# Squares taken one unit ahead, inverse roots spread over the scan, and gates stored in the scan's order

## The chip, the cores and the metric

The kernel runs on one core of a Trainium2 chip. The metric is the device time of one execution in microseconds. The times shown are the median of three runs; the profile is of one further execution, taken by the hardware profiler.

## What is computed

The input x is 16 sequences of 256 tokens with 256 features. The model has four parts in a row; the change lies in the first.

1. RMS norm of x, a causal convolution of 4 taps over the tokens with SiLU, projections to queries, keys and values of 16 heads of 16 features, and to two gates per head, beta and alpha. Then the gated delta rule, a recurrence over the tokens:

```
S = a[..., None, None] * S
pred = einsum('bhkv,bhk->bhv', S, k)
S = S + k[..., :, None] * (b[..., None] * (v - pred))[..., None, :]
o = einsum('bhkv,bhk->bhv', S, q)
```

2. An output projection, a second RMS norm, a gated MLP and a layer norm.
3. Cross attention to a context of 120 tokens per sequence, and a layer norm.
4. Eight experts, one for each token, and a layer norm.

## The kernel before, in words

The program is written by hand for five engines with semaphores; each engine runs its own list of instructions in order. There are three stages: `front_and_scan`, `scan_and_post`, and the experts.

**Units.** The work ahead of the recurrence is cut into NU = 16 units. A unit is 4 sequences of 64 tokens; U = 4 units cover all sequences for one part of 64 tokens, and there are PARTS = 4 parts. A unit goes through these steps: SyncE loads x (`load_rows`); ScalarE squares and sums it (line 638, into ss); GpSimd makes the inverse root (`inverse_rms`, lines 450 and 452); ScalarE scales x by it (line 645; VectorE does so for units 0 to 3, line 531); TensorE transposes; ScalarE writes the result with the norm's weight (line 666); TensorE convolves (line 795; VectorE for units 0 to 3); ScalarE applies SiLU (line 653); TensorE projects; ScalarE moves the projections to st and stores them to the DRAM tensor qkv (lines 678 and 680), then the gates to bst (line 690), and the gates are stored with four small DMAs (`store_gates`, line 342): by GpSimd for units 0 to 3, by ScalarE for the others. ScalarE's list is software-pipelined: `step(a, b, c)` treats the scale and transposition of unit a, the SiLU of unit b = a - 1 and the projections of unit c = a - 2.

**Raw loads.** SyncE's `load_raw(part, h)` brings keys, queries, gates and values of one part and one half h of the sequences from DRAM into the order of the scan, after it has waited for each of their stores. The gates take eight DMAs per half (line 379). For part 1 the two halves stand behind `load_rows` of units 9 and 10. The loads of parts 2 and 3 stand behind the 16 contexts (`contexts`, keys and values of the cross attention), and those behind unit 15.

**Lengths.** `lengths(some, h)` makes the inverse norms of keys and queries and the scales from the gates. It is shared by ScalarE (squares of keys and of queries, line 712; sigmoid, lines 703 and 704; roots) and VectorE (sums of the squares, line 559; products; reciprocals). `some` is 0 for part 0, 1 for part 1, 2 for parts 2 and 3.

**Scan.** VectorE walks the recurrence over 128 tokens at a time (jb = 0, then jb = 1), in CHUNKS = 16 chunks of R = 8 tokens. A token takes four instructions for each half of the sequences (lines 159, 170, 181, 191). At the sixth token of each chunk (u = 5) `next_scales` copies the next scales (line 125), so this copy marks the chunks in the trace. Beside it GpSimd reads out: `read_out(c, z, h)` covers four tokens of one half with one product (line 246), three folds (line 252) and one more (line 254). A chunk has four read-outs, two for each z, and one product of the queries (line 230). VectorE may overwrite the state of a slot only when GpSimd has read it eight tokens before (semaphore S_read, waited for at line 191 for every fourth token). VectorE's chunks 5 and 6 hold the sums of `lengths(1, h)`, the keys' from the second token on, and chunks 14 and 15 those of `lengths(2, h)`.

**Where the units lie.** GpSimd's list sets when a unit's inverse root is made, since it stands between read-outs. Written as (chunk, z), units 4 and 5 stand ahead of the scan; units 6 to 11 behind (0,0), (0,1), (1,0), (1,1), (2,0), (2,1); unit 12 behind (3,0); units 13, 14 and 15 behind (7,0), (7,1) and (8,0). ScalarE has `lengths(1, 0)` and `lengths(1, 1)` behind step 2U + 4 = 12.

Of the kernel before, what the change touches and what calls it, by code (L numbers as in the profile page):

```python
# [14 lines left out]
P = 128  # L15
# [7 lines left out]
NU = PARTS * U  # L23
R, Q, V, KN, KB = 8, 4, 4, 4, 2
# [239 lines left out]
def front_and_scan(nc, sem, w, k, s, arena):  # L264
# [4 lines left out]
    with ExitStack() as ctx:  # L269
# [6 lines left out]
        xt = sb("xt", [P, 2, 2, D])  # L276
        ss, ms, rstd = (sb(n, [P, 2, 2]) for n in ("ss", "ms", "rstd"))
# [23 lines left out]
        ct, cT = sb("ct", [CTX, 2, D]), sb("cT", [P, 2, G, CTX])  # L301
# [4 lines left out]
        pa = ps("pa", [P, G, 2 * TB])  # L306
        pc = pp[:, 0, :, 0:CTX]
# [5 lines left out]
        x_in, ct_in, kv_out = ([sem(f"f_{n}{i}") for i in range(2)] for n in ("x_in", "ct_in", "kv_out"))  # L313
# [18 lines left out]
        SETUPS = 13  # L332
        TAPS = KC * G
# [3 lines left out]
        def store_gates(eng, n):  # L337

            eng.wait_ge(evac_done, n * 4 + 4)
            for i in range(2):  # L340
                for g in range(G):
                    eng.dma_start(k["gates"][i, n, g].rearrange("a q h t -> h (a q) t"),
                                  bst[32 * i + g * H // G:32 * i + (g + 1) * H // G]).then_inc(gates_out[n >= U], 16)

        @block.sync
        def _(sp):
            def load_rows(n):

                part, u, s = n // U, n % U, n % 2
                if n >= 2:  # L350
                    sp.wait_ge(xn_done, (n - 1) * 2)
# [14 lines left out]
            def load_raw(part, h):  # L366
# [5 lines left out]
                for i, name, dst in ((1, "k", x["k"]), (0, "q", x["q"]), (3, None, None), (2, "v", x["vo"])):  # L372

                    if i == 3:
                        later = part > 0
                        sp.wait_ge(gates_out[later], 64 * (units - U * later))
# [50 lines left out]
        def _(pool):  # L427
# [18 lines left out]
            def inverse_rms(a):  # L446
                if a:
                    n, slot, m = a
                    pool.wait_ge(ss_done, (n + 1) * 2)
                    nc.gpsimd.tensor_tensor(ms[:, slot], ss[:, slot], k["eps"][:, 0], ALU.add).then_inc(rstd_done, 1)  # L450
                    pool.wait_ge(rstd_done, n * 2 + 1)
                    nc.gpsimd.tensor_tensor(rstd[:, slot], ms[:, slot], k["exponent"][:], ALU.pow).then_inc(rstd_done, 1)
# [1582 lines left out]
```

## Time and profile before

| | before |
|---|---|
| median of 3 runs | 1869.99 us |
| lowest and highest | 1865.32 and 1873.29 us |
| the profiled execution's own time | 1867.18 us |
| its span in the trace | 1865.5 us |
| TensorE busy | 1325.9 us, 71% |
| VectorE busy | 1254.0 us, 67% |
| GpSimd busy | 1000.8 us, 54% |
| ScalarE busy | 849.6 us, 46% |
| mean granted TensorE clock | 0.854 |

The span is the time from the first to the last instruction in the trace. Busy times are of one engine over the whole span, with stages of different limits in it, so they do not tell which engine sets the time of a stage. A row of the trace gives the start, the duration, the engine, the line, what is written and read, and in brackets how long the engine stood idle before it and what ended that. Consecutive instructions of one kind are merged into one row with a count. PE is TensorE, DVE VectorE, ACT ScalarE, POOL GpSimd; SPq and ACTq are DMA issues of SyncE and ScalarE.

### The profile page before, as it was taken

The numbers are of one execution on the slowest core, as the hardware profiler recorded it, in microseconds if no ns is written. First come the engines' busy times: TensorE is split into PE (matmuls) and PEld (weight loads), VectorE is DVE, ScalarE is ACT, GpSimd is POOL, SyncE is SP. The second block draws the span as 40 slices with busy tenths as digits, with TensorE's granted clock in tenths as the row PEclk, the third lists the DMA queues.
The fourth block names the chain that finished last, engine by engine and source line by source line (L and its number), as shares of the span: only waits on it lengthen the run. The fifth ranks groups of instructions, "written<-read, shape, count | busy, mean of one in ns | idle before, by whom it ended". The sixth has DMA issues, their size and how long they took to land. (4 is left out here: it accounts for less than half of the span.)

```text
span 1865.5 us, 32852 instructions
## 1 busy us (share of the span) xinstructions
PE 1325.9 (71%) x9000; PEld 1151.7 (62%) x9001; DVE 1254.0 (67%) x3301; ACT 849.6 (46%) x2808; POOL 1000.8 (54%) x1234
## 2 busy tenths in 40 slices
PE   6277106850036676766765899998489999999997
PEld 4265105630025465654654778876389999999997
DVE  3798999999988999999876144454434444443442
ACT  5433213442113665667766488887322322322332
POOL 3367868987669999998866324342111122122121
PEclk9689558885568878878877999998789999999999
DMA  5344001566031010100002111133130410411200
GB/s 139 74 102 111 12 6 42 143 173 95 23 120 38 23 33 18 32 27 27 28 27 84 57 42 52 54 120 120 40 103 21 154 48 22 158 42 45 77 17 7
DMA packets 182719, 119.29 MB, mean 64 GB/s; under 512 B 124849, under 2 KB 163560, under 8 KB 182120
## 3 DMA queue, kind: packets, MB, share of 16 engines
q1 hardware_dynamic: 119848, 90.98, 17.4%
q10 hardware_dynamic: 58864, 18.71, 4.0%
q0 software_dynamic: 3920, 8.60, 1.3%
q8 instruction: 34, 0.56, 0.1%
q14 instruction: 53, 0.43, 0.1%
HBM read 83.44 MB, written 35.74 MB: 64 GB/s over the span
## 5 line engine op out<-in xcount | busy, mean ns | idle before, releaser
L246 POOL TENSOR_TENSOR wt<-wt 128x1024 f32<-128x1024 f32 x128 | 301.5, 2355 | 53.9 <-DVE wt L191 46.9
L252 POOL TENSOR_TENSOR wt<-wt 128x512 f32<-128x512 f32 (+2 forms) x384 | 307.6, 801 | 30.1
L1942 PE MATMUL e_ph<-e_g,e_w 128*128 128x128 f32 x2496 | 285.2, 275 | 0.7 <-ACT e_g L1912 0.7
L1942 PEld LDWEIGHTS e_ph<-e_g,e_w 128*128 128x128 f32 x2496 | 281.9, 192 | 0.9 <-issue 0.9
L191 DVE SCALAR_TENSOR_TENSOR wt<-wt,scan 128x256 f32<-128x256 f32 x512 | 242.0, 473 | 18.0 <-POOL wt L246 13.4
L170 DVE TENSOR_REDUCE wt<-wt 128x16 f32<-128x272 f32 x512 | 219.2, 428 | 0.1
L181 DVE TENSOR_TENSOR scan<-wt,scan 128x256 f32<-128x256 f32 x512 | 215.0, 420 | 0.3
L159 DVE TENSOR_TENSOR wt<-wt,scan 128x256 f32<-128x256 f32 x512 | 210.1, 410 | 0.9 <-PEq L269 0.5
L1420 ACT ACTIVATE wt<-p_pX,p_mx 128x120 f32<-128x120 f32 x512 | 176.4, 387 | 71.9 <-DVE p_mx L1205 70.3
L1903 ACT ACTIVATE e_g<-e_ph,wt 128x128 f32<-128x128 f32 x156 | 48.7, 363 | 304.9 <-PE e_ph L1942 304.9
L1821 POOL TENSOR_TENSOR e_ve<-e_mv,eps 128x1 f32<-128x1 f32 x39 | 7.4, 190 | 327.1 <-DVE e_mv L1877 327.1
L1554 PE MATMUL p_pm<-p_w_mix,p_oT 128*128 128x256 f32 x128 | 43.7, 500 | 160.6 <-DMA p_oT<-o 129.9
L1953 PE MATMUL e_ph<-e_xT,e_w 128*128 128x128 f32 x1248 | 148.3, 278 | 0.6 <-DVE e_xT L1858 0.6
L1953 PEld LDWEIGHTS e_ph<-e_xT,e_w 128*128 128x128 f32 x1248 | 145.0, 195 | 1.0 <-issue 1.0
L782 PE MATMUL f_pT<-ident,f_xn 128*128 128x128 f32 x64 | 15.0, 377 | 171.9 <-ACT f_xn L645 157.9
L1554 PEld LDWEIGHTS p_pm<-p_w_mix,p_oT 128*128 128x128 f32 x128 | 30.8, 252 | 170.4 <-issue 162.0
L1205 DVE TENSOR_REDUCE p_mx<-p_pX 128x8 f32<-128x960 f32 x64 | 72.9, 1150 | 75.7 <-PE p_pX L1600 75.5
L1420 ACT ACTIVATION_READ_ACCUMULATOR wt<-p_pX,p_mx 128x1 f32 x512 | 119.9, 234 | 0.0
L782 PEld LDWEIGHTS f_pT<-ident,f_xn 128*128 128x128 f32 x64 | 9.7, 188 | 177.4 <-ACT f_xn L645 162.8
L1912 ACT ACTIVATE e_g<-e_ph,wt 128x128 f32<-128x128 f32 x312 | 97.4, 363 | 42.0 <-PE e_ph L1953 41.8
L1850 DVE COPY e_w<-wt 128x4096 f32 x39 | 89.5, 2295 | 27.3 <-issue 22.2
L1566 PE MATMUL p_pX<-p_hT,p_wg 128*128 128x256 f32 x320 | 94.8, 424 | 16.7 <-ACT wt L1420 16.6
(226 smaller groups left out, 2925.0 us busy)
## 6 DMA issues: line engine op xcount, KB each, us to landing
wt<-in_L_ffn_W SPq DMA_DIRECT2D x24, 1024.0 KB
qkv<-f_st ACTq DMA_DIRECT2D x48, 256.0 KB, 2.6
p_kE<-kE SPq DMA_DIRECT2D x16, 480.0 KB, 3.7
p_vP<-vP SPq DMA_DIRECT2D x16, 480.0 KB
wt<-qkv SPq DMA_DIRECT2D x12, 512.0 KB, 6.4
e_xt<-routed ACTq DMA_DIRECT2D x39, 130.0 KB, 2.1
f_xt<-in_x SPq DMA_DIRECT2D x32, 128.0 KB, 2.8
p_oT<-o SPq DMA_DIRECT2D x16, 256.0 KB
```

The source lines that it names most:

```text
L159: nc.vector.tensor_tensor(s["sk"][:, h, u % V, :, 0:HD], s["S"][:, h, (u - 1) % R], s["kn"][:, h, u % KN:u % KN + 1].to_broadcast([P, HD, ...
L170: nc.vector.tensor_reduce(s["w"][:, h], s["sk"][:, h, u % V], AX, ALU.add).then_inc(s["w_done"], 1)
L181: nc.vector.tensor_tensor(s["outer"][:], s["w"][:, h].rearrange("p (v o) -> p v o", o=1).to_broadcast([P, HD, HD]), s["kn"][:, h, u % KN:u ...
L191: nc.vector.scalar_tensor_tensor(s["S"][:, h, u], s["S"][:, h, (u - 1) % R], s["gate"][:, jb, h, 2, bass.ds(c * R + u, 1)], s["outer"][:], ...
L246: nc.gpsimd.tensor_tensor(x, s["S"][:, h, z * Q:(z + 1) * Q], s["qn"][:, h, z * Q:(z + 1) * Q].rearrange("p t (o d) -> p t o d", o=1).to_b ...
L252: nc.gpsimd.tensor_tensor(x[:, :, :, 0:half], x[:, :, :, 0:half], x[:, :, :, half:2 * half], ALU.add).then_inc(s["o_fold"][h], 1)
L1420: ins = nc.scalar.activation(pr[:, x // 2, head], scores(x)[:, y // 4, y % 4], ACT.Exp, bias=mx[:, x // 2, head:head + 1], accum_out=sm[:, ...
L1566: ins = nc.tensor.matmul(gu(i)[:, which], wt[:, g, i * P:(i + 1) * P], hT[:, g], start=(g == 0), stop=(g == G - 1))
L1850: nc.vector.tensor_copy(w2[:, s].rearrange("p c f -> p (c f)"), wt[:, bass.ds(at + W2_AT, C1 * F2)]).then_inc(w2_kept, 1)
L1912: nc.scalar.activation(g1[:, c], ph1[:, c // 2, c % 2], ACT.Gelu, bias=k["bias"][:, bass.ds(at + c * NE, 1)]).then_inc(g1_done, 1)
L1942: ins = nc.tensor.matmul(ph2[:, c // 2, c % 2], w2[:, s, i, c * P:(c + 1) * P], g1[:, i], start=(i == 0), stop=(i == C1 - 1))
L1953: ins = nc.tensor.matmul(ph1[:, c // 2, c % 2], w1[:, s, g, c * P:(c + 1) * P], xT[:, g], start=(g == 0), stop=(g == G - 1))
```

## The change

It has four parts.

- Squares go one unit ahead. A function `squares_of(n)` takes the place of the squares at the head of `step`; it is called for unit a + 1 behind the scaling of unit a. Its full-size output goes to a new PSUM tile `squared` and no longer to xn. The buffers of x and of its sums have XS = 3 slots in place of 2, and `load_rows` runs three units ahead. The context's buffer ct now lies in acc.
- Fewer inverse roots beside the scan's first chunks. Unit 4 stands behind (0,1), unit 5 behind (1,0), units 6 and 7 behind (2,0) and (2,1), unit 8 behind (3,0), units 9 and 10 behind (4,0) and (4,1), none in chunks 5 and 6, units 11 and 12 behind (7,0) and (7,1), unit 13 behind (8,0), units 14 and 15 behind (9,0) and (9,1).
- ScalarE's `lengths(1, 0)` and `lengths(1, 1)` come behind step 2U + 2 = 10.
- The DRAM tensor gates has its dimensions in the scan's order: eight stores of 4 KB for each unit, two loads of 64 KB for each half.

The core of the diff:

```diff
@@ store_gates
                 for g in range(G):
-                    eng.dma_start(k["gates"][i, n, g].rearrange("a q h t -> h (a q) t"),
-                                  bst[32 * i + g * H // G:32 * i + (g + 1) * H // G]).then_inc(gates_out[n >= U], 16)
+                    for a in range(2):
+                        eng.dma_start(k["gates"][i, n, a, g].rearrange("q h t -> h q t"),
+                                      bst[32 * i + g * H // G:32 * i + (g + 1) * H // G, 2 * a:2 * a + 2]).then_inc(gates_out[n >= U], 16)
@@ load_rows, load_raw
-                if n >= 2:
-                    sp.wait_ge(xn_done, (n - 1) * 2)
+                if n >= XS:
+                    sp.wait_ge(xn_done, (n - XS + 1) * 2)
...
                         for y in range(2):
-                            for pair in range(U):
-                                sp.dma_start(s["gate"][32 * pair:32 * pair + 32, jb, h, 1 + y, now],
-                                             k["gates"][y, rows.start + pair // 2, :, pair % 2].rearrange("g q h t -> g (q h) t")).then_inc(gate_in[h], 16)
+                            sp.dma_start(s["gate"][:, jb, h, 1 + y, now], k["gates"][y, rows].rearrange("u a g q h t -> (u a g q h) t")).then_inc(gate_in[h], 16)
@@ GpSimd
-            for n in range(U, U + 2):
-                inverse_rms((n, n % 2, n // 2))
...
-            with pool.Fori(0, half - 5) as c:
-                for z in range(R // Q):
-                    outputs(c, z)
-                    inverse_rms((c * 2 + (U + 2 + z), z, c + (U // 2 + 1)))
...
-            for c, z, n in ((half - 1, 0, NU - 3), (half - 1, 1, NU - 2), (half, 0, NU - 1)):
...
+            chunk(0, {1: (U, U)})
+            with pool.Fori(0, 2) as i:
+                chunk(i * 2 + 1, {0: (i * 3 + (U + 1), U + 1)})
+                chunk(i * 2 + 2, {0: (i * 3 + (U + 2), U + 2), 1: (i * 3 + (U + 3), U + 3)})
+            for c in range(MEASURE, MEASURE + 2):
+                chunk(c)
+            chunk(MEASURE + 2, {0: (NU - 5, NU - 5), 1: (NU - 4, NU - 4)})
+            ready(1)
+            chunk(MEASURE + 3, {0: (NU - 3, NU - 3)})
+            chunk(MEASURE + 4, {0: (NU - 2, NU - 2), 1: (NU - 1, NU - 1)})
@@ ScalarE
+            def squares_of(n):
+                act.wait_ge(x_in[n % XS], n // XS * 32 + 32)
+                if n >= 1:
+                    act.wait_ge(rstd_done, n * 2)
+                for q in range(2):
+                    nc.scalar.activation(squared[:, q], xt[:, n % XS, q], ACT.Square, accum_out=ss[:, n % XS, q:q + 1]).then_inc(ss_done, 1)
...
+                if a is not None and a + 1 < (U if a < U else NU):
+                    squares_of(a + 1)
...
-            units(U, NU, {2 * U + 4: (*lengths(1, 0), *lengths(1, 1))})
+            units(U, NU, {2 * U + 2: (*lengths(1, 0), *lengths(1, 1))})
```

GpSimd's list where the front's units end and the scan's first read-out begins, before. L450 and L452 are the two instructions of one inverse root, L342 is a gate store, and the branch and what follows belong to the first read-out.

```order
L342 DMA gates<-f_bst 8x4x64 [waits f_evac_done]
L342 DMA gates<-f_bst 8x4x64 x3
L450 TENSOR_TENSOR f_ms<-f_ss,eps 128x2 [waits f_ss_done]
L452 TENSOR_TENSOR f_rstd<-f_ms,exponent 128x2 [waits f_rstd_done]
L450 TENSOR_TENSOR f_ms<-f_ss,eps 128x2 [waits f_ss_done]
L452 TENSOR_TENSOR f_rstd<-f_ms,exponent 128x2 [waits f_rstd_done]
L477 UNCONDITIONAL_BRANCH [waits f_rn_done,f_raw_in_q1,f_raw_in_q0]
```

The same place now, and behind it the end of the second pair of read-outs of chunk 0 with the first inverse root (L452 and L454).

```order
L347 DMA gates<-f_bst 8x2x64 [waits f_evac_done]
L347 DMA gates<-f_bst 8x2x64 x7
L231 TENSOR_TENSOR wt<-f_raw_q,f_rq 128x256 [waits f_rn_done,f_raw_in_q1,f_raw_in_q0]
...
L253 TENSOR_TENSOR wt<-wt 128x64x2 [waits s_o_fold1]
L255 TENSOR_TENSOR f_vo<-wt 128x4x16 [waits s_o_fold1]
L452 TENSOR_TENSOR f_ms<-f_ss,eps 128x2 [waits f_ss_done]
L454 TENSOR_TENSOR f_rstd<-f_ms,exponent 128x2 [waits f_rstd_done]
L485 UNCONDITIONAL_BRANCH
```

The inverse roots of units 4 and 5 no longer stand ahead of the scan, and that of unit 4 has four read-outs in front of it.

ScalarE's list ahead of `lengths(1, 0)`, before: step 12, from the squares of unit 12 to the first square of the keys (L712).

```order
L638 ACTIVATE f_xn,f_ss<-f_xt 128x256 [waits f_T_done,f_x_in0]
L638 ACTIVATE f_xn,f_ss<-f_xt 128x256
L678 ACTIVATE f_st<-f_pp 128x2x2x128 [waits f_out_q,f_proj_done]
L680 DMA qkv<-f_st 128x8x64 [waits f_evac_done]
L645 ACTIVATE f_xn<-f_xt,f_rstd 128x256 [waits f_rstd_done]
...
L690 ACTIVATE f_bst<-f_pp 48x256 [waits f_gates_out1,f_proj_done]
L342 DMA gates<-f_bst 8x4x64 [waits f_evac_done]
L342 DMA gates<-f_bst 8x4x64 x3
L712 ACTIVATE wt<-f_raw_k 128x16x64 [waits f_fold_done,f_raw_in_k0]
```

The same now: step 10, from the scaling of unit 10 to the first square of the keys (L715).

```order
L646 ACTIVATE f_xn<-f_xt,f_rstd 128x256 [waits f_T_done,f_rstd_done]
L646 ACTIVATE f_xn<-f_xt,f_rstd 128x256
L635 ACTIVATE f_squared,f_ss<-f_xt 128x256 [waits f_rstd_done,f_x_in2]
L635 ACTIVATE f_squared,f_ss<-f_xt 128x256
L656 ACTIVATE f_xc<-f_pa,f_cb 128x256 [waits f_proj_done,f_conv_done]
...
L693 ACTIVATE f_bst<-f_pp 48x256 [waits f_gates_out1,f_proj_done]
L347 DMA gates<-f_bst 8x2x64 [waits f_evac_done]
L347 DMA gates<-f_bst 8x2x64 x7
L715 ACTIVATE wt<-f_raw_k 128x16x64 [waits f_fold_done,f_raw_in_k0]
```

The squares of the next unit (here 11) now stand behind the scaling, with a wait for that unit's x, and the keys' square stands behind the step of unit 10.

## Rows read from the trace of the kernel before

**Rows 1.** Page, busy tenths in 40 slices of 46.6 us, VectorE.
```profile
DVE  3798999999988999999876144454434444443442
```
**Rows 2.** Waits, 62 to 460 us: who waited for whom, us in total, times, longest.
```profile
POOL f_ms L450 <- ACT f_xn L638: 41.7, 10, 16.2
...
DVE wt L191 <- POOL wt L246: 11.6, 6, 3.6
...
DVE wt L191 <- POOLq L462: 4.5, 1, 4.5
```
**Rows 3.** Timeline of VectorE, the copies that mark chunks.
```profile
62.01 0.20 DVE L125 COPY scan<-wt 128x32 f32<-128x32 f32 x1 [0.23 <-DVE wt L550]
84.39 0.19 DVE L125 COPY scan<-wt 128x32 f32<-128x32 f32 x1
191.81 0.18 DVE L125 COPY scan<-wt 128x32 f32 x1
332.15 0.18 DVE L125 COPY scan<-wt 128x32 f32 x1
355.97 0.18 DVE L125 COPY scan<-wt 128x32 f32 x1
```
**Rows 4.** Timeline of GpSimd: read-outs of chunk 0, an inverse root, the queries' product.
```profile
78.38 2.36 POOL L246 TENSOR_TENSOR wt<-wt 128x1024 f32<-128x1024 f32 x1 [8.23 <-DVE wt L191]
89.15 0.19 POOL L450 TENSOR_TENSOR f_ms<-f_ss,eps 128x2 f32<-128x2 f32 x1
90.31 2.35 POOL L246 TENSOR_TENSOR wt<-wt 128x1024 f32<-128x1024 f32 x1 [0.19 <-DVE wt L191]
...
243.12 0.76 POOL L230 TENSOR_TENSOR wt<-f_raw_q,f_rq 128x256 f32 x1
```
**Rows 5.** Timeline of ScalarE, steps 11 and 12 and the lengths of part 1.
```profile
165.39 0.42 ACT L638 ACTIVATE f_xn<-f_xt 128x256 f32<-128x256 f32 x1 [4.82 <-DMA f_xt<-in_x]
182.04 0.91 ACT L645 ACTIVATE f_xn<-f_xt,f_rstd 128x256 f32<-128x256 f32 x2 [0.61 <-POOL f_rstd L452]
187.15 0.84 ACT L653 ACTIVATE f_xc<-f_pa,f_cb 128x256 f32<-128x256 f32 x2 [4.21 <-PE f_pa L795]
192.79 1.06 ACT L712 ACTIVATE wt<-f_raw_k 128x1024 f32<-128x1024 f32 x1 [1.48 <-issue]
```
**Rows 6.** Timeline of VectorE, first sums of the keys for parts 0, 1 and 2.
```profile
39.99 1.74 DVE L559 TENSOR_TENSOR wt<-wt 128x512 f32<-128x512 f32 x4 [6.28 <-ACT wt L712]
203.75 4.77 DVE L559 TENSOR_TENSOR wt<-wt 128x512 f32<-128x512 f32 x4
439.36 5.71 DVE L559 TENSOR_TENSOR wt<-wt 128x1024 f32<-128x1024 f32 x4
```
**Rows 7.** Gate DMAs by tile: duration of an issue min/median/max in ns, and time to landing.
```profile
L379 SPq DMA_DIRECT2D wt<-gates x64: 591/592/2232, 38.6 to 446.2; - x64
L342 ACTq DMA_DIRECT2D gates<-f_bst x48: 277/323/1789, 102.4 to 345.1; - x48
L342 POOL DMA_DIRECT2D gates<-f_bst x16: 544/544/820, 26.7 to 46.5; - x16
...
DMA to landing us min/median/max: 1.7/3.3/4.4
```
**Rows 8.** Timeline of ScalarE: gates ahead of the scan, and unit 15 to the last lengths.
```profile
57.55 0.26 ACT L703 ACTIVATE wt<-wt 128x64 f32<-128x64 f32 x1 [0.61 <-DMA wt<-gates]
317.58 0.91 ACT L645 ACTIVATE f_xn<-f_xt,f_rstd 128x256 f32<-128x256 f32 x2 [0.61 <-POOL f_rstd L452]
345.52 0.37 ACT L745 ACTIVATE f_cT<-f_pp 128x240 f32<-128x240 f32 x1 [1.64 <-issue]
420.87 1.91 ACT L712 ACTIVATE wt<-wt 128x2048 f32<-128x2048 f32 x1 [16.39 <-DMA wt<-qkv]
```
**Rows 9.** Timeline of SyncE's DMA issues, raw loads of parts 2 and 3.
```profile
404.92 2.67 SPq L383 DMA_DIRECT2D wt<-qkv  x2
407.64 6.13 SPq L379 DMA_DIRECT2D wt<-gates  x8
```

More of the change, by code:

```diff
@@ L275, in front_and_scan @@
         cw, cb = sb("cw", [P, G, KC]), sb("cb", [P, G])
[L276 to L277 removed]
+        xt = sb("xt", [P, XS, 2, D])
+        ss, ms, rstd = (sb(n, [P, XS, 2]) for n in ("ss", "ms", "rstd"))
         xn = sb("xn", [P, 2, 2, D])
@@ L312, in front_and_scan @@
         BIT, ODD, EVEN, NORM1, BIAS_K = 1, 2, 3, 4, 4 + G
-        x_in, ct_in, kv_out = ([sem(f"f_{n}{i}") for i in range(2)] for n in ("x_in", "ct_in", "kv_out"))
+        x_in = [sem(f"f_x_in{i}") for i in range(XS)]
+        ct_in, kv_out = ([sem(f"f_{n}{i}") for i in range(2)] for n in ("ct_in", "kv_out"))
         out = [sem(f"f_out_{n}") for n in "qkv"]
@@ L444, in _, with inverse_rms @@
             pool.wait_ge(set_up, SETUPS)
[L446 to L452, printed above, removed]
+            def inverse_rms(n, slot):
+                pool.wait_ge(ss_done, n * 2 + 2)
+                nc.gpsimd.tensor_tensor(ms[:, slot], ss[:, slot], k["eps"][:, 0], ALU.add).then_inc(rstd_done, 1)
+                pool.wait_ge(rstd_done, n * 2 + 1)
+                nc.gpsimd.tensor_tensor(rstd[:, slot], ms[:, slot], k["exponent"][:], ALU.pow).then_inc(rstd_done, 1)
             for step in range(U + 3):
                 if step < U:
-                    inverse_rms((step, step % 2, step // 2))
+                    inverse_rms(step, step % XS)
                 if step >= 3:
                     store_gates(pool, step - 3)
-            for n in range(U, U + 2):
-                inverse_rms((n, n % 2, n // 2))
             for h in range(2):
@@ L475, in _, with chunk @@
             ready(0)
-            half = CHUNKS // 2
-            with pool.Fori(0, half - 5) as c:
+            def chunk(c, units={}):
                 for z in range(R // Q):
                     outputs(c, z)
-                    inverse_rms((c * 2 + (U + 2 + z), z, c + (U // 2 + 1)))
-            outputs(half - 5, 0)
-            inverse_rms((NU - 4, 0, NU // 2 - 2))
-            outputs(half - 5, 1)
-            with pool.Fori(half - 4, half - 1) as c:
-                for z in range(R // Q):
-                    outputs(c, z)
-            for c, z, n in ((half - 1, 0, NU - 3), (half - 1, 1, NU - 2), (half, 0, NU - 1)):
-                if c == half:
-                    ready(1)
-                outputs(c, z)
-                inverse_rms((n, n % 2, n // 2))
-            outputs(half, 1)
-            with pool.Fori(half + 1, CHUNKS) as c:
-                for z in range(R // Q):
-                    outputs(c, z)
+                    if z in units:
+                        n, slot = units[z]
+                        inverse_rms(n, slot % XS)
+            chunk(0, {1: (U, U)})
[8 more added lines that the diff above has]
+            chunk(MEASURE + 4, {0: (NU - 2, NU - 2), 1: (NU - 1, NU - 1)})
+            with pool.Fori(MEASURE + 5, CHUNKS) as c:
+                chunk(c)
         @block.vector
@@ L700, in gates @@
                 def gates():
-                    act.wait_ge(gate_in[h], 32 * U * parts)
+                    act.wait_ge(gate_in[h], 32 * parts)
                     beta, alpha = (s["gate"][:, jb, h, 1 + i, now] for i in range(2))
@@ L724, in units @@
             def units(first, last, between):
+                squares_of(first)
                 for at in range(first, last + 2):
```

27 lines of the change are left out of this document (12 added, 15 removed).

## The prediction

> **What bounds the kernel now.** I read the page first for where the time lies, then the waits of the stretch that the change touches, then the timelines of VectorE, GpSimd and ScalarE in it. Squares, inverse roots and gates are used up to about 500 us; what follows only starts sooner or later by what this part gains or loses. In slices 2 to 10 (47 to 466 us) VectorE is busy at 7 to 9 tenths or more [rows 1]: the scan's own instructions set the pace. From 332.15 to 355.97 a chunk takes 23.82 us with no wait at all [rows 3], and this is what the scan can do at best.
>
> Earlier it does worse. The copy of chunk 0 stands at 84.39 and that of chunk 4 at 191.81 [rows 3]: 107.4 us for four chunks, where 4 x 23.82 are 95.3, so 12.1 us are lost. The waits say to whom: VectorE's state update stood idle 11.6 us for a read-out of GpSimd, and once 4.5 us for GpSimd's list, which had not yet come to its first read-out [rows 2]. Together 16.1 us. GpSimd is late because its inverse roots wait for ScalarE's squares, 41.7 us in 10 waits [rows 2], while the read-outs behind them stand still. So there is something to win: 16.1 us.
>
> How much GpSimd can do: two read-outs and nothing else take 10.8 us (78.38 to 89.15), an inverse root with its two instructions about 0.95 us (89.15 to 90.31, less a wait of 0.19), and the queries' product, once a chunk, 0.76 us [rows 4]. Four read-outs, the product and 1.5 roots are 21.5 + 0.8 + 1.4 = 23.7 us: as long as VectorE's chunk. Two roots, as before, make it 24.2, and they waited besides.
>
> **The change, step by step.** Times are of the profiled execution, with the span at 1865.5 and its own time at 1867.18 us.
>
> *1. The opening.* The gates of unit 3 come to GpSimd's queue as eight stores and not four, 0.544 us each on that queue [rows 7]: 4 x 0.544 = 2.2 us more. Units 1 to 3 each wait in bst for the stores of the one before, so it can be 2.2 to 6.5 us. Against that stand two loads for eight at 0.592 us [rows 7], 3.6 us less in front of the last gate to land. ScalarE's sigmoid waited 0.61 us for these gates at 57.55 [rows 8], so no more than 0.6 can be won. Bounds -0.6 and +2.9; I take +1.9, towards the upper end, because the stores of units 1 to 3 form a chain. The scan starts at 62.0 + 1.9 = 63.9.
>
> *2. Waits of the scan.* Without the roots of units 4 and 5 ahead of it GpSimd is ready, and the 4.5 us go. With squares one unit ahead the roots find their sums, and with 1.5 per chunk GpSimd keeps pace; the 11.6 us go too. Chunk 4 then ends at 63.9 + 5 x 23.82 = 183.0.
>
> *3. A new wait: the lengths of part 1.* VectorE wants the keys' squares of part 1 in chunk 5 behind its first two tokens of 2.98 us, at 183.0 + 6.0 = 189.0. ScalarE makes them only behind step 10. Step 10 starts with the scaling of unit 10, which needs the root of unit 10, and this root now stands behind the read-outs of (4,1). Those need the last state of chunk 4: 183.0 + 10.8 + 0.9 = 194.7. That alone is past 189.0. Then the rest of the step: before, from the scaling at 182.04 to the keys' square at 192.79 it took 10.75 us [rows 5]. To this come four more stores on ScalarE at 0.323 us [rows 7], 1.3 us; the tail copies of a unit below 12, 0.3; and what ScalarE is late itself, since the roots of units 9 and 10 are half a chunk, 11.9 us, apart, and a step with eight stores takes longer than that (10.75 + 1.3 + 0.3, and up to 2 to the next scaling), 3 us more. Besides, the squares of unit 11 now stand ahead of the SiLU of unit 9 and wait for x, whose load stands on SyncE's queue behind the raw loads of units 6 and 7. The same load made ScalarE wait 4.82 us at 165.39 [rows 5], and I take 3 us here. Sum: 194.7 + 10.75 + 1.3 + 0.3 + 3 + 3 = 213.1, and 1.1 for the square itself: 214.2. ScalarE waited 4.21 us for TensorE's convolution at 187.15 [rows 5]; TensorE will have had more idle time ahead of this one, and I add a third of that, 1.3 us, as an estimate: 215.5. So VectorE waits about 26 us. Against the sums' start at 203.75 before [rows 6] they are 11.8 us later: the 16.1 us won are gone, and 12 more.
>
> A part comes back. The four sums took 4.77 us at 203.75, while the same four took 1.74 at 39.99, when GpSimd was idle [rows 6]; those of the queries and later ones were stretched likewise. After a wait of 26 us GpSimd has nothing left to read out, and the first sums run free: I take 4 us. The Trainium skill (SBUF — State Buffer, SBUF: two separate sides) states an exclusive lock between VectorE instructions with two SBUF inputs and GpSimd's: the loser stands for the other's whole instruction. By it all eight sums of this half would run free, some 5.5 us, and the sum would be 1.5 us lower. With the row at 203.75 the rule agrees.
>
> Step 3 in all: +11.8 - 4 = **+7.8 us** against before, at the end of chunk 6. Bounds: ScalarE never late by itself, no wait for x and a fast TensorE, 208: +4.3 less 5.5, -1; everything slow and no sum shortened, 219: +15.
>
> *4. A second new wait: the lengths of parts 2 and 3.* Unit 15 has its root now behind (9,1), before behind (8,0). The copy of chunk 9 was at 332.15 [rows 3], and two more tokens of 2.98 us end the chunk at 338.1. The root comes at 338.1 + 10.8 + 0.9 = 349.8; with ScalarE late by 1.9 the scaling of unit 15 is at 351.7, before 317.58 [rows 8]. That is 34.1 us later. From there to the first context ScalarE needed 27.9 us (to 345.52 [rows 8]); it now has 3 x 4 more stores at 0.323, 4 us. The contexts' own 59.4 us (345.52 to 404.92) are unchanged, so SyncE's raw loads start at 404.92 [rows 9] + 38.1 = 443.0. The keys' square followed 16 us behind this start, at 420.87 [rows 8]; the eight gate loads of 6.13 us between [rows 9] shrink to two of 1.2, so I take 12 us: 455.0, and 1.9 for the square, 456.9. VectorE wanted it at 439.36 [rows 6]. Here 17.5 us of wait, less 3 us because four sums of 5.71 us [rows 6] run free: **+14.5 us**. Bounds: 8 (ScalarE not late, stores half as dear, loads landing in 9) and 24 (loads landing in 16, contexts slower beside a fuller scan, nothing back). Before, the square was 16.6 us early (439.36 - 422.78), which is what hid all this.
>
> *Costed at nothing:* the output into PSUM (same instruction, same width), the third slot of x, ct in acc (acc is idle by then), six fewer loads per half in the later raw loads apart from the 4 us above, and SyncE's stores of the scan's outputs, which wait for GpSimd.
>
> **Sum.** 7.8 + 14.5 = +22.3 us on 1867.18: 1889.5. The median of the runs is 2.8 us above the profiled execution; half of that added gives **1891 us**.
>
> **A rule against the stores.** Rows first: the stores on GpSimd's queue are issued 0.544 us apart, and each lands 3.3 us after its own issue, 4.4 at most [rows 7]. Were four of them served one after the other, the fourth would land some 13 us after the first, 11 after its issue; so they overlap. The Trainium skill (DMA: Bandwidth & Descriptors, Anatomy of one DMA) gives a fixed cost of about 2.0 us for each DMA, nearly all of it completion. If that were paid one after the other, eight small stores would cost 8 us more per unit by that page and the opening 24 us instead of 1.9.
>
> **The rivals.**
> - *Only the first wait.* The contexts go faster or the raw loads land sooner, and the square of parts 2 and 3 is in time or nearly so. For it: 16.6 us of lead before. Against it: unit 15 is a chunk and a half later. About +8: 1877. Chance 0.12.
> - *Faster: squares in time.* ScalarE's chain from unit 10's root to the keys' square stays ahead of VectorE. Then the 16.1 us go for +1.9 in the opening: -14, 1854. It decides at 189.0 for part 1 and 439.4 for parts 2 and 3. For it: 41.7 us of waits for squares vanish. Against it: the root of unit 10 alone comes at 194.7. Chance 0.06.
> - *The stores are serial.* From the fifth store on each waits for the one before: 4 x 3.3 us [rows 7] per unit, three units, +40 in the opening, 1930. Chance 0.02, since four stores did not behave so.
> - *Both waits at their upper bounds:* 15 + 24, 1906 to 1909. Chance 0.12.
> - *The forecast,* both waits, +6 to +31: chance 0.68.
>
> **Numbers.** The range is 1872 to 1908: at the lower end the bounds -1 and 8 meet (+7, on 1867), at the upper the bounds 15 and 24 with the median's 2.8. A measurement of this kernel tells a change from none at about 0.5%, 9.4 us. Faster by more: 0.06. Slower by more: the forecast nearly whole, the upper case, the stores and a third of the first rival, 0.86. The rest, 0.08, is the same.
>
> **What would show it.** In the profile after: the waits of VectorE at line 191 for GpSimd near 0 where they were 16.1; copies of chunks 0 to 4 23.8 us apart; the root of unit 4 near 99 us; one long idle time of VectorE, near 26 us, ahead of the first sum of part 1, ended by ScalarE's square, and one near 17 us at chunk 14; the gate loads as pairs on SyncE's queue. I am wrong if either long wait is missing, if VectorE still waits for read-outs, or if the scan starts after 66 us.

## The result, and the profile after

| | before | after |
|---|---|---|
| median (4 runs each, same chip) | 1867.65 us | 1896.9 us |
| lowest and highest | 1863.27 and 1873.29 us | 1895.7 and 1902.47 us |
| span in the trace | 1865.5 us | 1895.2 us |
| ratio, 95% interval | | 1.0162, 1.0131 to 1.0193 |

The changed kernel is slower by 29.3 us in the medians and by 29.7 in the spans. Its line numbers are a little higher: the copy of the scales is L126 (before 125), the state update L192 (191), the read-out's product L247 (246), an inverse root L452 and L454 (450 and 452), the squares of x L635 (638), the scaling L646 (645), the gate stores L347 (342), the gate loads L383 (379), the squares of keys L715 (712). The sums are L559 in both.

The page after, the span and VectorE's and GpSimd's rows of 40 slices, here of 47.4 us each (before [rows 1]):

```profile
span 1895.2 us, 32818 instructions
...
DVE  3899399996988999999876125344344444434442
...
POOL 4499268985669999888776524432112211221121
```

The fifth digit (190 to 237 us) reads 3 for VectorE and 2 for GpSimd, where their neighbours are 9 and 9, and 9 and 6: there both stood still for most of the slice. The tenth (426 to 474 us) reads 6 and 5. The waits from 62 to 470 us, 10 us further than in [rows 2], since the same work ends later; pieces of the list (engine and line, what it waited for, us in all, times, the longest):

```profile
ACT f_xn L646 <- POOL f_rstd L454: 92.2, 5, 34.6
...
POOL wt L247 <- issue: 54.2, 4, 32.1
DVE wt L559 <- ACT wt L715: 46.0, 2, 30.1
...
ACT f_squared L635 <- DMA f_xt<-in_x: 8.4, 1, 8.4
```

The waits of VectorE's state update and of GpSimd's inverse roots are gone from this list. In their place VectorE waits twice, 46.0 us in all, for ScalarE's squares of keys. ScalarE itself waits 92.2 us for inverse roots, where it was 50.4 before: it is let go late. VectorE's timeline (start, duration, line, what is written and read, how often, and in brackets the idle time before it) gives the places, to be read beside [rows 3] and [rows 6]:

```profile
65.51 0.20 DVE L126 COPY scan<-wt 128x32 f32<-128x32 f32 x1 [0.23 <-DVE wt L550]
83.32 0.18 DVE L126 COPY scan<-wt 128x32 f32<-128x32 f32 x1
107.10 0.18 DVE L126 COPY scan<-wt 128x32 f32 x1
...
220.68 1.73 DVE L559 TENSOR_TENSOR wt<-wt 128x512 f32<-128x512 f32 x4 [30.14 <-ACT wt L715]
...
466.44 2.74 DVE L559 TENSOR_TENSOR wt<-wt 128x1024 f32<-128x1024 f32 x4 [15.91 <-ACT wt L715]
```

The scan starts at 65.51 (before 62.01), its chunks are 23.8 us apart, and then come a wait of 30.14 us ahead of the first sum of part 1 and one of 15.91 at chunk 14. The first sum stands at 220.68 where it stood at 203.75, the later one at 466.44 where it stood at 439.36.

Where the time is lost, by the start of the same piece of work in both traces:

| piece of work | before | after | difference |
|---|---|---|---|
| first copy, scan starts | 62.01 | 65.51 | +3.5 |
| copy of chunk 5 | 224.99 | 236.41 | +11.4 |
| copy of chunk 8 | 308.32 | 319.46 | +11.1 |
| copy of chunk 14, the last of the first 128 tokens | 460.17 | 484.27 | +24.1 |
| first copy of the other 128 tokens | 505.39 | 529.48 | +24.1 |
| last copy of the scan | 958.1 | 985.8 | +27.7 |
| first transposition of the experts | 1356.27 | 1386.27 | +30.0 |

So 24.1 of the 30 us are lost in the stretch that the change touches, and about 6 later, where the code is the same; the traces of the experiments show below how much that later part varies by itself.

### The profile page after: what moved, and what is told of

It reads as the page before. It is cut to its first block and busy times, and to the rows that moved or that the text cites. A ratio compares the mean times of both kernels' runs of the same rounds, so it can differ in the third digit from the quotient of the medians.

```text
span 1895.2 us, 32818 instructions
## 1 busy us (share of the span) xinstructions
PE 1330.9 (70%) x9000; PEld 1154.0 (61%) x9001; DVE 1247.7 (66%) x3301; ACT 848.8 (45%) x2808; POOL 1006.9 (53%) x1250
## 3 DMA queue, kind: packets, MB, share of 16 engines
q1 hardware_dynamic: 119976, 90.98, 17.4%
## 5 line engine op out<-in xcount | busy, mean ns | idle before, releaser
L247 POOL TENSOR_TENSOR wt<-wt 128x1024 f32<-128x1024 f32 x128 | 301.2, 2353 | 106.5 <-issue 54.4
L253 POOL TENSOR_TENSOR wt<-wt 128x512 f32<-128x512 f32 (+2 forms) x384 | 306.0, 797 | 30.1
L192 DVE SCALAR_TENSOR_TENSOR wt<-wt,scan 128x256 f32<-128x256 f32 x512 | 241.3, 471 | 1.8 <-POOL wt L247 1.8
L786 PE MATMUL f_pT<-ident,f_xn 128*128 128x128 f32 x64 | 15.9, 395 | 206.7 <-ACT f_xn L646 193.1
L1582 PE MATMUL p_py<-p_wd,p_prod 128*128 128x256 f32 x384 | 100.7, 418 | 10.4 <-POOL p_prod L1130 5.5
```

The source lines that it names most:

```text
L192: nc.vector.scalar_tensor_tensor(s["S"][:, h, u], s["S"][:, h, (u - 1) % R], s["gate"][:, jb, h, 2, bass.ds(c * R + u, 1)], s["outer"][:], ...
L247: nc.gpsimd.tensor_tensor(x, s["S"][:, h, z * Q:(z + 1) * Q], s["qn"][:, h, z * Q:(z + 1) * Q].rearrange("p t (o d) -> p t o d", o=1).to_b ...
L253: nc.gpsimd.tensor_tensor(x[:, :, :, 0:half], x[:, :, :, 0:half], x[:, :, :, half:2 * half], ALU.add).then_inc(s["o_fold"][h], 1)
L1582: ins = nc.tensor.matmul(py[:, q], prod[:, i, q * P:(q + 1) * P], wd[:, i], start=(i == 0), stop=(i == IC - 1))
```

## The experiments

The ratios are against the kernel before on the same chip: the first four share one comparison (before at 1865.97 us), the last four another (before at 1867.69 us). The changed kernel's own 1.0162 comes from a third.

**Old gates.** After, with the gates' layout, four stores for each unit and eight loads for each half put back.

```diff
-                    for a in range(2):
-                        eng.dma_start(k["gates"][i, n, a, g].rearrange("q h t -> h q t"), bst[..., 2 * a:2 * a + 2])
+                    eng.dma_start(k["gates"][i, n, g].rearrange("a q h t -> h (a q) t"), bst[...])
...
-                            sp.dma_start(s["gate"][:, jb, h, 1 + y, now], k["gates"][y, rows]...)
+                            for pair in range(U):
+                                sp.dma_start(s["gate"][32 * pair:32 * pair + 32, jb, h, 1 + y, now], k["gates"][y, rows.start + pair // 2, :, pair % 2]...)
```

> The changed kernel with the gates stored and loaded as before: four stores per unit, eight loads per half. Theory (the places of the inverse roots make the two long waits; the stores only move the opening): the scan starts near 62.0 us where it started at 65.5, ScalarE's steps are 1.3 us shorter, the raw loads 4 us longer; VectorE still waits 27 to 31 us ahead of the first sum of part 1 and 14 to 20 us at chunk 14; time 3 to 5 us below the changed kernel, ratio to before 1.013 to 1.015. Rival (the doubled stores keep ScalarE busy and are the main cause): the two waits shrink by half or more, ratio below 1.007.

Measured: 1889.38 us, ratio 1.0119 (1.0072 to 1.0166). VectorE's timeline, with L560 and L716 in place of L559 and L715:

```profile
217.89 1.74 DVE L560 TENSOR_TENSOR wt<-wt 128x512 f32<-128x512 f32 x4 [30.90 <-ACT wt L716]
...
461.29 2.74 DVE L560 TENSOR_TENSOR wt<-wt 128x1024 f32<-128x1024 f32 x4 [13.48 <-ACT wt L716]
```

Both waits stay, 30.90 and 13.48 us. The scan starts at 61.92, 3.6 us sooner. The second wait is 2.4 us shorter, which fits the 12 more stores on ScalarE's queue between unit 12 and the contexts that are gone here. The ratio is slightly under the 1.013 to 1.015 that I gave, with an interval that holds both. The gates cost the opening and part of the second wait; the two waits are there without them.

**Old places.** After, with the inverse roots and ScalarE's lengths where they were before; squares ahead and new gates stay.

```diff
+            for n in range(U, U + 2):
+                inverse_rms(n, n % XS)
...
+            for c in range(3):
+                chunk(c, {z: (c * 2 + U + 2 + z,) * 2 for z in range(2)})
+            chunk(3, {0: (NU - 4, NU - 4)})
...
-            units(U, NU, {2 * U + 2: (*lengths(1, 0), *lengths(1, 1))})
+            units(U, NU, {2 * U + 4: (*lengths(1, 0), *lengths(1, 1))})
```

> The changed kernel with the inverse roots and the lengths of part 1 in the places of before; squares one unit ahead, three slots of x and the new gates stay. Theory (GpSimd waits because ScalarE takes 14 to 16 us for a unit while two roots come per chunk, every 11.9 us): taking squares ahead does not free GpSimd; VectorE still loses 12 to 20 us in chunks 0 to 4, the long waits of 30 and 16 us are gone, time 1871 to 1880, ratio 1.001 to 1.007. Rival (the squares' place behind the stores was the cause): VectorE's waits for read-outs are near 0 in chunks 1 to 4, and the time is near 1859, ratio 0.995.

Measured: 1867.4 us, ratio 1.0008 (0.9988 to 1.0029). The waits of its scan:

```profile
DVE wt L192 <- POOL wt L247: 7.7, 2, 4.1
DVE wt L559 <- ACT wt L715: 4.2, 1, 4.2
DVE wt L192 <- POOLq L464: 2.0, 1, 2.0
```

The two long waits are gone, and one of 4.2 us is left ahead of the first sum. The state update still waits 9.7 us, where it was 16.1 [rows 2]. Less of it stayed than the 12 to 20 us I had given, and ratio and time lie just below my 1.001 to 1.007 and 1871 to 1880 us. Squares one unit ahead do free part of the scan, 6.4 us of these waits; the later start of the scan (64.70 for 62.01) and the wait of 4.2 us take it back.

**Places alone.** Before, with only GpSimd's new places (no root ahead of the scan; unit 10 behind (4,1), unit 15 behind (9,1)) and the lengths behind step 10; no squares ahead, old gates.

```diff
-            for n in range(U, U + 2):
-                inverse_rms((n, n % 2, n // 2))
...
+            chunk(0, {1: 4})
+            chunk(1, {0: 5})
+            chunk(2, {0: 6, 1: 7})
+            chunk(3, {0: 8})
+            chunk(4, {0: 9, 1: 10})
+            chunk(5)
+            chunk(6)
+            chunk(7, {0: 11, 1: 12})
+            ready(1)
+            chunk(8, {0: 13})
+            chunk(9, {0: 14, 1: 15})
...
-            units(U, NU, {2 * U + 4: (*lengths(1, 0), *lengths(1, 1))})
+            units(U, NU, {2 * U + 2: (*lengths(1, 0), *lengths(1, 1))})
```

> The kernel before with nothing but the inverse roots and the lengths of part 1 in the changed places; squares at the head of a step, two slots of x, old gates. Theory: the places alone bring the two long waits, 24 to 31 us ahead of the first sum of part 1 and 10 to 18 us at chunk 14, and take away the 16 us of waits for read-outs but for a few us where two roots are 11.9 us apart; ratio 1.010 to 1.016. Rival (squares ahead or the gates are the cause of the slowdown): ratio at or below 1.000.

Measured: 1891.13 us, ratio 1.0131 (1.0093 to 1.017). VectorE's timeline (the sums are L557 here, the squares L710):

```profile
213.38 1.73 DVE L557 TENSOR_TENSOR wt<-wt 128x512 f32<-128x512 f32 x4 [25.18 <-ACT wt L710]
...
464.98 2.74 DVE L557 TENSOR_TENSOR wt<-wt 128x1024 f32<-128x1024 f32 x4 [21.42 <-ACT wt L710]
```

This part of the change makes both waits by itself, 25.18 and 21.42 us. The second is longer than the 15.91 of the whole change, and longer than the 10 to 18 us that I had expected: the old eight gate loads are on that path again, and that there are no squares ahead may have its share; the two are not separated.

**x first.** After, with the raw loads of the second half of part 1 behind the load of x for unit 11.

```diff
-                if n in (2 * U + 1, 2 * U + 2):
-                    load_raw(1, n - 2 * U - 1)
+                if n in (2 * U + 1, 2 * U + 3):
+                    load_raw(1, (n - 2 * U - 1) // 2)
```

> The changed kernel with the raw loads of the second half of part 1 behind load_rows of unit 11 and not of unit 10, so that x of unit 11 does not wait for the gates of unit 7. Theory: ScalarE's wait of 8.4 us for this x at 211 us is gone, the SiLU behind it then waits for TensorE, and VectorE's first long wait falls from 30.1 to 26 or 27 us; the time falls by the same 3 to 4 us, since nothing else ends there: ratio 1.013 to 1.015. Rival (the wait for x is covered by something else that ends as late, such as the raw keys): the long wait stays at 30 us and the time does not move.

Measured: 1890.83 us, ratio 1.0136 (1.0097 to 1.0174). After has 1.0162 in its own comparison, and the two intervals overlap: whether the whole kernel gains is not shown. The spans of the two traces, 1885.6 and 1895.2 us, don't settle it either, because the traced execution of this run is the fastest of its four (1887.32 to 1897.04). What the trace does show is the wait. VectorE's timeline:

```profile
215.10 1.74 DVE L559 TENSOR_TENSOR wt<-wt 128x512 f32<-128x512 f32 x4 [25.20 <-ACT wt L715]
```

The wait goes from 30.14 to 25.20, a little further than the 26 to 27 I gave. ScalarE's timeline says why it is not the whole 8.36 us of its wait for x:

```profile
199.84 0.91 ACT L646 ACTIVATE f_xn<-f_xt,f_rstd 128x256 f32<-128x256 f32 x2 [0.52 <-ACT f_st L681]
200.66 0.37 ACT L635 ACTIVATE f_squared<-f_xt 128x256 f32<-128x256 f32 x1
...
206.64 0.84 ACT L656 ACTIVATE f_xc<-f_pa,f_cb 128x256 f32<-128x256 f32 x2 [5.09 <-PE f_pa L799]
```

The squares run at once, and then the SiLU waits 5.09 us for TensorE's convolution: x had covered that wait, and 3.3 us were its own. From the scaling of unit 10 to the keys' square it takes 14.2 us (199.84 to 214.01) in place of 17.4; the rest of the gain comes from the scaling, which is 2.3 us sooner.

**Early.** After, with what the first four suggest. The theory says that the roots are too late, not too many: unit 10 now stands behind (3,0) in place of (4,1), unit 15 behind (8,0) in place of (9,1), the others one to one and a half chunks sooner too, unit 11 three. The semaphore that lets VectorE overwrite the state is released first, ahead of the roots of units 4 and 5.

```diff
             for h in range(2):
                 pool.sem_inc(s["S_read"][h], 2)
                 pool.sem_inc(s["o_done"][h], 1)
+            for n in range(U, U + 2):
+                inverse_rms(n, n % XS)
...
+            chunk(0, {1: (6, 6)})
+            chunk(1, {0: (7, 7)})
+            chunk(2, {0: (8, 8), 1: (9, 9)})
+            chunk(3, {0: (10, 10)})
+            chunk(4, {0: (11, 11)})
+            chunk(5, {})
+            chunk(6, {1: (12, 12)})
+            chunk(7, {0: (13, 13), 1: (14, 14)})
...
+            chunk(8, {0: (15, 15)})
```

The roots of units 4 and 5 stand ahead of the scan again, but behind the release, and x goes first as in the run above.

> The changed kernel with the roots two units earlier: the scan's semaphores are released first, then units 4 and 5 get their roots while GpSimd would only wait for the scan's first four tokens; unit 6 behind (0,1), 7 (1,0), 8 (2,0), 9 (2,1), 10 (3,0), 11 (4,0), 12 (6,1), 13 (7,0), 14 (7,1), 15 (8,0); x of unit 11 ahead of the raw loads as in the run before. Theory: both long waits are gone or under 3 us and VectorE does not wait for read-outs; the scan starts at 65, the first sum of part 1 stands near 191 (203.75 before), the saved 12 to 13 us stay; time 1852 to 1858, ratio 0.992 to 0.996. Rival (squares ahead, the third slot and the new gates cost something besides the places): ratio at or above 1.000.

Measured: 1853.3 us, ratio 0.9919 (0.9903 to 0.9935), a hair under my 0.992 to 0.996. VectorE has no wait for ScalarE's squares or GpSimd's read-outs. Its timeline (L561 are the sums):

```profile
189.99 4.58 DVE L561 TENSOR_TENSOR wt<-wt 128x512 f32<-128x512 f32 x4
...
422.61 5.71 DVE L561 TENSOR_TENSOR wt<-wt 128x1024 f32<-128x1024 f32 x4
```

No bracket: the sums find their squares. They take 4.58 and 5.71 us again, since GpSimd works beside them.

**Early, old gates.** The same with the gates as before (both diffs above together).

> The run before with the gates stored and loaded in the old form. Theory: the opening is 3 us shorter (scan starts at 62) and nothing else is on the path, since the raw loads of parts 2 and 3 have room; ratio 0.990 to 0.994, below that of the new gates by 0.001 to 0.002. Rival (the eight loads per half bring back a wait at chunk 14): ratio the same as with the new gates or above.

Measured: 1848.62 us, ratio 0.9897 (0.988 to 0.9915), just under my 0.990 to 0.994 and the best of all. VectorE's timeline:

```profile
186.88 4.59 DVE L562 TENSOR_TENSOR wt<-wt 128x512 f32<-128x512 f32 x4
...
419.52 5.70 DVE L562 TENSOR_TENSOR wt<-wt 128x1024 f32<-128x1024 f32 x4
```

Both stand 3.1 us sooner than in the run above, as the start of the scan does (61.92 and 64.98): up to here the new gates cost the opening and nothing else.

**Before, early.** Before, with GpSimd's list alone changed: release first, and the places of the two runs above but for units 11 to 15.

```diff
+            chunk(0, {1: 6})
+            chunk(1, {0: 7})
+            chunk(2, {0: 8, 1: 9})
+            chunk(3, {0: 10})
...
+            chunk(6, {0: 11})
+            chunk(7, {0: 12, 1: 13})
+            ready(1)
+            chunk(8, {1: 14})
+            chunk(9, {0: 15})
...
-            units(U, NU, {2 * U + 4: (*lengths(1, 0), *lengths(1, 1))})
+            units(U, NU, {2 * U + 2: (*lengths(1, 0), *lengths(1, 1))})
```

> The kernel before, with squares where they were, and only GpSimd's list changed: semaphores released first, units 4 and 5 right behind, unit 6 behind (0,1), 7 (1,0), 8 (2,0), 9 (2,1), 10 (3,0), 11 (6,0), 12 (7,0), 13 (7,1), 14 (8,1), 15 (9,0), the lengths of part 1 behind step 10. Theory (the order of the roots is what counts, squares ahead are not needed for it): scan starts at 62, no waits for read-outs over 2 us in all, first sum of part 1 near 188, a wait of 0 to 6 us at chunk 14; ratio 0.990 to 0.995. Rival (only squares ahead free GpSimd): waits for read-outs of over 8 us remain, ratio above 0.997.

Measured: 1853.82 us, ratio 0.9917 (0.9902 to 0.9933). One wait for squares is left in its list:

```profile
DVE wt L559 <- ACT wt L712: 4.9, 1, 4.9
```

It stands at chunk 14, where unit 15 behind (9,0) is a little late. Without squares ahead GpSimd still waits 34.2 us for them, but that hides beside the scan: squares ahead are not what the gain needs. How the gain divides is told by the next run: of the 13.9 us in the medians the release brings 9.8 by itself, and the places, with the lengths two steps earlier, 4.1 more.

**Release alone.** Before, with only the release moved ahead of the roots of units 4 and 5.

```diff
-            for n in range(U, U + 2):
-                inverse_rms((n, n % 2, n // 2))
             for h in range(2):
                 pool.sem_inc(s["S_read"][h], 2)
                 pool.sem_inc(s["o_done"][h], 1)
+            for n in range(U, U + 2):
+                inverse_rms((n, n % 2, n // 2))
```

> The kernel before with one change: the scan's semaphores are released ahead of the roots of units 4 and 5 and not behind them. Theory (GpSimd's waits in chunks 1 to 4 are set by ScalarE's pace of 13 to 16 us per unit, which does not start sooner): the 4.5 us at the scan's first token are gone but come back as waits for read-outs in chunks 2 to 4, 16 to 17 us in all as before; ratio 0.999 to 1.001. Rival (the waits add up independently): the time falls by 4.5 us, ratio 0.9975.

Measured: 1857.92 us, ratio 0.9956 (0.9938 to 0.9974). Two of its waits, and GpSimd's timeline at the root of unit 6 and at the last root of the first group (that of unit 12):

```profile
DVE wt L191 <- POOL wt L246: 7.0, 4, 3.5
...
POOL f_ms L450 <- ACT f_xn L638: 36.6, 10, 16.1
```

```profile
84.92 0.20 POOL L450 TENSOR_TENSOR f_ms<-f_ss,eps 128x2 f32<-128x2 f32 x1
...
171.91 0.20 POOL L450 TENSOR_TENSOR f_ms<-f_ss,eps 128x2 f32<-128x2 f32 x1 [2.15 <-ACT f_xn L638]
```

My theory for this run falls. It said that the 4.5 us go and come back as waits of the loop between ScalarE and GpSimd. But the state update waits 7.0 us, not 16.1 or the 11.6 that would be left, and the gain is 9.8 us in the medians, more than the 4.5 that the rival gave it. The trace says how. Before, the root of unit 6 stood at 89.15 [rows 4]; here at 84.92, since it follows the first read-out, and that follows the scan. So ScalarE starts on unit 6 4.2 us sooner and the whole loop moves with the scan; the last root of this group, at 171.91, stands 9.1 us sooner than before (181.03). That the rest, from 4.2 to 9.1, comes from the read-outs that no longer queue behind a waiting root is my reading of it, not shown by a run.

## Why the prediction was right, and where not

The sign, the mechanism and both places were right; 1891 was forecast and 1896.9 measured, inside the range. Against its own base the forecast was +22.3, the spans give +29.7. Several terms were off, and in steps 3 and 4 their errors offset each other: that part of the agreement is luck.

**Step 1, the opening: mis-sized.** Forecast +1.9 with an upper bound of 2.9, measured +3.5; the run with old gates gives 3.6 back. The chain of stores through bst was named, but priced at a fraction. ScalarE's timeline shows two of its links:

```profile
42.01 0.38 ACT L693 ACTIVATE f_bst<-f_pp 48x256 f32<-48x256 f32 x1 [4.62 <-DMA gates<-f_bst]
...
49.84 0.38 ACT L693 ACTIVATE f_bst<-f_pp 48x256 f32<-48x256 f32 x1 [3.84 <-DMA gates<-f_bst]
```

Before, the same two waits were shorter:

```profile
38.64 0.38 ACT L690 ACTIVATE f_bst<-f_pp 48x256 f32<-48x256 f32 x1 [1.69 <-DMA gates<-f_bst]
...
44.22 0.38 ACT L690 ACTIVATE f_bst<-f_pp 48x256 f32<-48x256 f32 x1 [0.90 <-DMA gates<-f_bst]
```

So each link grew by 2.9, more than four issues of 0.544 [rows 7]. The same paragraph had put the chain at up to 6.5 us and then an upper bound of 2.9; it should have carried the 6.5. How two links of 2.9 become 3.5 at the scan's start was not taken apart.

**A rule against the stores.** The rows of the gates' operations after (duration ns least, median, most; first and last start), and the time from issue to landing:

```profile
L347 ACTq DMA_DIRECT2D gates<-f_bst x96: 271/321/1538, 149.0 to 394.1; - x96
L347 POOL DMA_DIRECT2D gates<-f_bst x32: 557/557/818, 25.6 to 54.4; - x32
L383 SPq DMA_DIRECT2D wt<-gates x16: 325/433/2622, 41.9 to 479.2; - x16
...
DMA to landing us min/median/max: 1.6/3.3/5.4
```

The last row mixes stores with the gate loads, whose longest time is the 5.4. GpSimd's stores alone:

```profile
DMA to landing us min/median/max: 1.7/3.5/4.9
```

Twice the stores, and the median to landing is 3.5 us for 3.3 [rows 7], the longest 4.9 for 4.4: they overlap, and the rival of +40 is out. The price is 0.557 us of GpSimd's queue and 0.321 of ScalarE's for each. The fixed cost of about 2.0 us that the Trainium skill (DMA: Bandwidth & Descriptors, Anatomy of one DMA) gives each DMA is thus paid beside the others' here, and the opening's 3.5 us are far from the 24 that it would make in series.

**Step 2, the scan's waits: right.** No state update waits for a read-out, the chunks are 23.8 us apart where 23.82 was said, and the root of unit 4 is at 99.69 where 99 was said. GpSimd's timeline at the root of unit 4 and of unit 10, and the wait behind it:

```profile
99.69 0.19 POOL L452 TENSOR_TENSOR f_ms<-f_ss,eps 128x2 f32<-128x2 f32 x1
...
195.97 0.20 POOL L452 TENSOR_TENSOR f_ms<-f_ss,eps 128x2 f32<-128x2 f32 x1
...
229.77 2.35 POOL L247 TENSOR_TENSOR wt<-wt 128x1024 f32<-128x1024 f32 x1 [32.10 <-issue]
```

**Step 3, the wait of part 1: right in kind, 30.1 us for about 26.** VectorE was ready at 220.68 - 30.14 = 190.5 (189.0 and the opening's 1.6), and the root of unit 10 ended at 196.95, two instructions from 195.97, where 194.7 was said. ScalarE's timeline, the scaling of unit 6 and then from the scaling of unit 10 to the square:

```profile
136.96 0.91 ACT L646 ACTIVATE f_xn<-f_xt,f_rstd 128x256 f32<-128x256 f32 x2 [12.65 <-POOL f_rstd L454]
...
202.18 0.91 ACT L646 ACTIVATE f_xn<-f_xt,f_rstd 128x256 f32<-128x256 f32 x2 [0.52 <-ACT f_st L681]
...
211.44 0.39 ACT L635 ACTIVATE f_squared<-f_xt 128x256 f32<-128x256 f32 x1 [8.36 <-DMA f_xt<-in_x]
...
219.59 1.06 ACT L715 ACTIVATE wt<-f_raw_k 128x1024 f32<-128x1024 f32 x1 [2.88 <-issue]
```

The scaling follows the root's end by 5.2 us where 3 were said: ScalarE's steps are 16 us apart (scalings of units 7 to 10 at 153.69, 170.12, 186.60, 202.18), not 12.4 to 14.4. Here the path of the prediction was off in one point. The root of unit 10 had been there for 5.2 us when ScalarE came to it, and none of the scalings of units 7 to 10 waited for its root. The last root that ScalarE waited for is unit 6's, at 136.96; from there its own four steps of 16.3 us set the time. So it is the late start of the whole chain, from unit 4 on, that makes the wait, and not the place of unit 10 alone. In the run *Early* the last such wait is that of unit 8, at 135.95, so ScalarE is two units further at the same time, and its square for the keys stands at 177.81. From the scaling to the square it takes 17.4 us; the terms for it, 10.75 + 1.3 + 0.3 + 3 + 1.3, are 16.65. That is near, but by two errors that offset: the wait for x was 8.36 for 3, and the 4.21 and 1.3 us for TensorE's convolution were not paid on top, because x covered them. Two waits in a row on one engine, of which the second runs down during the first, were added where the longer counts; putting x first showed it (5.09 us for TensorE as soon as x is there). So 2.2 us of the root, 2.2 of ScalarE's lateness and 0.8 of the step, 5.2 in all, make the sum start at 220.68 and not 215.5. SyncE's queue shows what stood ahead of that load:

```profile
197.18 0.55 SPq L386 DMA_DIRECT2D f_raw_k<-qkv  x1
197.78 2.49 SPq L386 DMA_DIRECT2D f_raw_q<-qkv  x1
204.54 0.80 SPq L383 DMA_DIRECT2D wt<-gates  x2
205.38 0.52 SPq L386 DMA_DIRECT2D f_vo<-qkv  x1
205.95 4.83 SPq L358 DMA_DIRECT2D f_xt<-in_x  x6
```

The queue stood from 200.27 to 204.54 ahead of the gate loads, which want unit 7's gates in DRAM (ScalarE stored them from 197.72 on), and x was behind them. Of what comes back the forecast took 4 us. From the first sum to the copy of chunk 5 it is 21.24 us before (203.75 to 224.99) and 15.73 now (220.68 to 236.41): 5.5 back. That is what the rule of the lock gave, which I had set aside for 4: the Trainium skill (SBUF — State Buffer, SBUF: two separate sides) and the trace agree here. In all the step, with the opening, makes +11.4 at chunk 5 and +11.1 at chunk 8 against 7.8: some 3.4 more, of which 1.6 is the opening.

**Step 4, the wait of chunk 14: right, 15.9 us for 17.5.** Unit 15 is scaled at 363.77, where 351.7 + 7.8 were said: 4.3 us late, of which 3.4 came with step 3. Yet the raw loads start at 451.71, only 0.9 later than the 450.8 that were said: from the scaling to them 91.3 us were forecast and 87.9 measured, and that offsets most of the late scaling. The square stands at 464.50 where 462.8 were said, and VectorE wanted it at 450.5 where 447.2 were said; both late, they make the wait come out near. The rows:

```profile
363.77 0.91 ACT L646 ACTIVATE f_xn<-f_xt,f_rstd 128x256 f32<-128x256 f32 x2 [0.52 <-ACT f_st L681]
...
464.50 1.91 ACT L715 ACTIVATE wt<-wt 128x2048 f32<-128x2048 f32 x1 [13.24 <-DMA wt<-qkv]
```

```profile
451.71 2.61 SPq L386 DMA_DIRECT2D wt<-qkv  x2
454.37 3.10 SPq L383 DMA_DIRECT2D wt<-gates  x2
```

The two gate loads were taken as 1.2 us and hold the queue for 3.10. The difference grows from 11.1 at chunk 8 to 24.1 at the copy of chunk 14, 13.0 us where 14.5 were said: 15.9 of wait less 3.0 of sums that run free (3 was said). Both terms together: 24.1 measured, 22.3 forecast.

**What the sum lacked.** The first lines of the working say that what follows "only starts sooner or later" and put it at nothing. From 529 us on nothing is changed, and still, in this trace, 3.6 us are lost up to the end of the scan and 2.3 from there to the experts. The copies of the other 128 tokens (count, duration in ns least, median, most, first and last start):

```profile
L125 DVE COPY scan<-wt x16: 178/182/195, 505.4 to 958.1; 128x32 f32<-128x32 f32 x10, 128x32 f32 x6
```

```profile
L126 DVE COPY scan<-wt x16: 175/182/194, 529.5 to 985.8; 128x32 f32<-128x32 f32 x10, 128x32 f32 x6
```

The first is before, 452.7 us from its first to its last copy, the second after, 456.3. In that stretch the scan shares VectorE with the attention, and the two lists are woven in an order that was not moved. TensorE's granted clock is the same over its two parts, 0.76 and 0.84 in both kernels, and the last 510 us (the experts) agree to 0.3 us. Whether the change costs these 5.9 us is not shown. All ten traces of this document have the same code there, and from the first of these copies to the last they take 452.3 us (places alone; early with old gates), 452.7 (before; release alone), 453.5, 454.5, 455.0, 455.7, 456.3 (after) and 458.8 (old gates), and from there to the experts 397.4 to 400.8. They are in no order of how late the scan is, and executions of before alone differ by 12 us (1860.46 to 1872.63). On the other hand the interval of the ratio is 24.5 to 36.0 us, a little above the 24.1 of the touched stretch, so a part may be real. It stays open.

**The rivals.** *Faster, squares in time:* its deadline of 189.0 was missed by 30 us; but in the early runs the same deadline was met, and they came at 1853.3, and 1848.62 with the old gates, against its 1854. The rival's price was right; this change's places don't meet its condition. *Only the first wait:* the 15.9 at chunk 14 rules it out. *Serial stores:* out by the landing times. *Both waits at their upper bounds:* no, +11.1 and +13.0 for 15 and 24. The ends of the stated range, 1872 and 1908, don't follow exactly from its own bounds, which give 1874 and 1909; nothing hangs on it.

## What to carry to other kernels

A small step that is moved later in an engine's in-order list, to take its load off one moment, delays all that hangs on it: compute when the last consumer down the chain wants its data, and move no step so far that the chain behind it ends past that (here 189 and 439 us). Count the whole chain from its first delayed link: the engine behind it may then need its own time for each further step, 16 us here, however early the later roots are. With most roots one to one and a half chunks sooner, and x ahead of the raw loads, +1.6% became -0.8%, and with the old stores -1.0%. Look first for what an engine could release at once: in the kernel before, moving the release of the scan's semaphores ahead of a wait that it does not need was worth 0.4% by itself, more than the places and the earlier lengths added to it (0.2%).

## What was not expected of the hardware

- Sums of VectorE with both inputs in SBUF are stretched when GpSimd works beside them: four of 128x512 take 4.77 us beside GpSimd [rows 6] and 1.73 while it is idle; four of 128x1024 take 5.71 and 2.74. This fits the exclusive lock that the Trainium skill (SBUF — State Buffer, SBUF: two separate sides) states for instructions with two inputs in SBUF. The scan's own products aren't stretched, though GpSimd is busy 84% of the time beside them: in before from 230 to 440 us, 133 each of lines 159 and 181, they take 401 to 423 and 408 to 429 ns. They read only one tensor of SBUF; the other, the keys, lies in `scan`, which the kernel allocates in PSUM. Size is not what decides: a product of 128x64 with both inputs in SBUF (line 543) takes 0.23 us at 58.07, where GpSimd is idle, and 0.69 at 221.41, while 34 products of 128x64 with one input in PSUM (line 135) take 253 to 272 ns from 230 to 440 us. Nor is it the broadcast of an operand, which lines 159, 181 and 135 have: the state update (line 191) has none, reads the state in SBUF and the outer product in PSUM, and takes 461 to 483 ns, 134 times. What is left, and fits all of these rows, is where the second input lies.
- Two gate loads hold SyncE's queue 0.80 us at 204.54, and 2.72 to 3.10 us each time among the raw loads of parts 2 and 3 (3.10 at 454.37): the same kind of issue cost up to four times as much at another place. What makes the difference no run here tells.
